# Attention probability as a difference of two exponentials, and expert routing work moved from VectorE to GpSimd, in a fused two-layer block kernel

## The reference

```python
# layer 0, attention over 7x7 windows of 8x8 tokens: every window attends to 4 windows (256 keys)
attn = einsum('bhnsd,bhnkd->bhnsk', q * scale, key_g)      # 64 queries x 256 keys, 8 heads
score, index = top_k(attn, 32)                             # the 32 best of 256 keys
out = einsum('bhnsk,bhnskd->bhnsd', softmax(score), v_sel) # + a 3x3 depthwise convolution of v
x = x + out @ out_w.T + out_b
# layer 0, experts on t = x
n = layernorm(t); probs = softmax(n @ router_w.T)
rw, re = top_k(probs, 2); rw = rw / max(rw.sum(), 1e-12)
t = t + n + sum_e combine[:, e] * (gelu(n @ w1[e] + b1[e]) @ w2[e] + b2[e])
# layer 1: 3x3 convolution of layernorm(x) with +-1 weights, then 8 experts, top 2, weights not renormalised
```

## Time and profile before

| | us |
|---|---|
| runs without profile, median of 3 | 6441.68 |
| the profiled execution's own time | 6440.11 |
| its span, first to last instruction | 6438.2 |
| VectorE busy | 5596.4 (87%) |
| TensorE matmul busy | 4737.3 (74%) |
| GpSimd busy | 4425.8 (69%) |
| ScalarE busy | 4054.4 (63%) |

### The profile page before, as it was taken

How to read it: one execution, slowest core, us unless ns; L and a number is a source line. 1 busy time by engine, 2 the same in 40 slices (tenths; PEclk the granted TensorE clock), 3 DMA queues, 4 the chain that set the end, 5 groups by cost and what they waited for, 6 DMA issues and landing times.

```text
span 6438.2 us, 135940 instructions
## 1 busy us (share of the span) xinstructions
PE 4737.3 (74%) x26938; PEld 2880.6 (45%) x26938; DVE 5596.4 (87%) x24453; ACT 4054.4 (63%) x10222; POOL 4425.8 (69%) x3986
## 2 busy tenths in 40 slices
PE   3566777777777777777777777777777777777776
PEld 1333444444444444444444444444444444444444
DVE  1999999988989998999989898989999899999941
ACT  2455666666666666666666666666666666666643
POOL 1667776767677776767677677767776777777742
PEclk9666767777777777777777777777777777777777
DMA  4111111111111111111111111111111111111100
GB/s 75 39 31 42 34 40 34 40 32 42 30 41 34 39 35 34 40 32 43 32 42 30 40 36 36 38 33 40 32 43 31 43 31 32 30 30 34 33 11 10
DMA packets 585501, 229.09 MB, mean 36 GB/s; under 512 B 481152, under 2 KB 580224, under 8 KB 584576
## 3 DMA queue, kind: packets, MB, share of 16 engines
q1 hardware_dynamic: 584576, 219.25, 15.4%
HBM read 150.14 MB, written 68.80 MB: 34 GB/s over the span
## 4 chain that ended last, share of the span: by engine, by line
PE 29%; ACT 18%; issue 16%; DVE 15%; POOL 12%; ACTq 0%; DVEq 0%; POOLq 0%; DMA 0%; SPq 0%
DVE b_v L452 7%; POOL b_r L502 5%; PE y_ps L685 4%; DVE b_r L463 4%; PE h_ps L611 4%; POOL c_h L762 4%; ACT b_x L478 3%; PE a_ps L666 3%; PE pT_ps L524 3%; PE o_ps L545 2%; ACT b_e L485 2%; ACT L737 2%; PE h_ps L666 2%; POOL b_rec L493 2%; ACT L478 2%
## 5 line engine op out<-in xcount | busy, mean ns | idle before, releaser
L463 DVE MATCH_REPLACE8 b_r<-b_v,b_r 128x256 f32<-128x256 f32 x4704 | 1879.1, 416 | 0.0
L502 POOL TENSOR_SCALAR b_r<-b_r,b_rec 128x256 f32<-128x256 f32 x1568 | 1777.1, 1147 | 119.6 <-POOL b_rec L493 119.6
L452 DVE MAX8 b_v<-b_r 128x8 f32<-128x256 f32 x4704 | 1649.2, 418 | 0.0
L524 PE MATMUL pT_ps<-k_ident,b_e 128*128 128x128 f32 x3136 | 669.9, 352 | 776.3 <-ACT b_pT L532 688.3
L493 POOL TENSOR_TENSOR b_rec<-b_den,k_mone 128x4 f32<-128x4 f32 x392 | 400.5, 1022 | 1153.5 <-ACT b_x L478 1150.2
L762 POOL TENSOR_TENSOR c_h<-c_h,c_cb 128x448 f32<-128x448 f32 x672 | 760.9, 1133 | 503.9 <-ACT c_cb L739 503.0
L524 PEld LDWEIGHTS pT_ps<-k_ident,b_e 128*128 128x128 f32 x3136 | 472.6, 180 | 1161.2 <-issue 1136.2
L510 POOL TENSOR_TENSOR b_e<-b_e,b_r 128x1024 f32<-128x1024 f32 x392 | 923.5, 2356 | 18.0 <-POOL b_r L502 14.4
L685 PE MATMUL y_ps<-k_w,c_h 128*112 128x64 f32 x5376 | 776.1, 298 | 181.1 <-POOL c_h L762 177.9
L685 PEld LDWEIGHTS y_ps<-k_w,c_h 128*112 128x112 f32 x5376 | 706.5, 210 | 404.1 <-issue 403.0
L452 DVE MAX8 b_v<-b_s 128x8 f32<-128x256 f32 x1568 | 551.1, 415 | 318.0 <-POOL b_e L510 201.2
(11 more groups left out here) (146 smaller groups left out, 7904.9 us busy)
## 6 DMA issues: line engine op xcount, KB each, us to landing
q_d<-a_qe SPq DMA_DIRECT2D x56, 448.0 KB, 4.2
b_k<-k_d SPq DMA_DIRECT2D x1568, 16.0 KB, 2.0
b_v<-v_d SPq DMA_DIRECT2D x1568, 16.0 KB, 2.0
b_q<-q_d SPq DMA_DIRECT2D x392, 64.0 KB, 2.1
c_win<-vpad_d SPq DMA_DIRECT2D x56, 145.0 KB, 2.8
c_hm<-cpad_d SPq DMA_DIRECT2D x56, 145.0 KB, 2.3
vpad_d<-a_vT SPq DMA_DIRECT2D x56, 116.0 KB, 3.7
c_win<-vpad_d SPq DMA_DIRECT2D x56, 116.0 KB, 2.7
```

The costliest lines, as they stand in the source:

```text
L452: top = dve.max(out=b_v8[p][:, t, 8 * rnd:8 * rnd + 8], in_=src[:, t, :])
L463: last = dve.match_replace(out=b_r[p][:, t, :], in_to_replace=b_v8[p][:, t, 8 * rnd:8 * rnd + 8], in_values=src[:, t, :], imm_value=GONE)
L502: last = pool.tensor_scalar(out=b_r[p][:, t, :], in0=b_r[p][:, t, :], scalar1=GONE, scalar2=b_rec[p][:, t:t + 1], op0=ALU.is_le, op1=ALU.mult)
L524: last = pe.transpose(pT_ps[:, col:col + 128], b_e[p][:, t, c * 128:(c + 1) * 128], k["ident"][:, :])
```

## The change

Five things are done.

1. In the attention, GpSimd's mask and its product go. Instead ScalarE takes the exponential also of `b_r`, in which the 32 chosen scores stand at -3e38 and so give 0 (`act_rest`, two halves of two heads), and GpSimd subtracts this from the exponential of all scores, in two halves (`pool_prob`). The division by the sum moves behind the product with v: TensorE spreads `b_rec` into 128 further columns of `o_ps`, ScalarE copies 256 columns instead of 128, and GpSimd multiplies once per strip (step NORM).
2. In the slot's order on ScalarE, `act_exp` of the next region now ends the slot, `act_turn`, `act_rest`, `act_scores`, `act_turn`, `act_sum` begin it, and the strip steps with a fraction under 0.2 stand behind these. TensorE's order follows it.
3. The sum `tok = x + pr` (step ADD) and the norm of the experts' input run on GpSimd.
4. The router on VectorE is now four MAX8 and four MATCH_REPLACE8 on 14 elements (8 logits, and 6 large fillers so that only the best two logits are replaced). GpSimd subtracts the maximum, ScalarE takes 64 exponentials a token instead of 32, and GpSimd makes the weights with ten small instructions (step 4).
5. `PLACES` moves steps accordingly.

```diff
         def dve_select(dve, tau, r):
-            dve.wait_ge(b_prob, reg + 1)
+            dve.wait_ge(b_prob, 2 * reg + 2)
+            dve.wait_ge(b_sum, reg + 1)
...
+        def act_exp(act, tau, r):
+            act.wait_ge(b_max, reg + 1)
+            act.activation(b_nm[p][:, :], b_v8[p][:, :, 0], ACT.Copy, scale=-1.0).then_inc(b_neg, 1)
+            act.wait_ge(b_neg, reg + 1)
+            for t in range(HP):
+                last = act.activation(b_e[p][:, t, :], b_s[p][:, t, :], ACT.Exp, bias=b_nm[p][:, t:t + 1])
+            last.then_inc(b_exp, 1)
+        def act_rest(act, tau, r):
+            for half in range(2):
+                act.wait_ge(b_sel, 2 * reg + half + 1)
+                for t in range(2 * half, 2 * half + 2):
+                    last = act.activation(b_r[p][:, t, :], b_r[p][:, t, :], ACT.Exp, bias=b_nm[p][:, t:t + 1])
+                last.then_inc(b_rest, 1)
...
-            for t in range(HP):
-                last = pool.tensor_scalar(out=b_r[p][:, t, :], in0=b_r[p][:, t, :], scalar1=GONE, scalar2=b_rec[p][:, t:t + 1],
-                                          op0=ALU.is_le, op1=ALU.mult)
+        def pool_prob(pool, tau, r):
+            for half in range(2):
+                pair = slice(2 * half, 2 * half + 2)
+                if half == 0:
+                    pool.wait_ge(b_exp, reg + 3)
+                pool.wait_ge(b_rest, 2 * reg + half + 1)
+                pool.tensor_tensor(out=b_e[p][:, pair, :], in0=b_e[p][:, pair, :], in1=b_r[p][:, pair, :],
+                                   op=ALU.subtract).then_inc(b_prob, 1)
...
+            for t in range(HP):
+                pe.matmul(o_ps[32 * t:32 * t + VH, 128:256], b_rec[r % 2][:, t:t + 1].broadcast_to([128, VH]), k["ident"][:, :],
+                          start=True, stop=True)
...
+            if step == NORM:
+                pool.wait_ge(b_att, NWIN * (s + 1) + 1)
+                pool.tensor_tensor(out=b_at[i][:, 0:2], in0=b_at[i][:, 0:2], in1=b_at[i][:, 2:4], op=ALU.mult).then_inc(b_nrm, 1)
+            if step == ADD:
+                pool.tensor_tensor(out=D["tok"][i][:, :, :], in0=D["x"][i][:, :, :], in1=D["pr"][:, :, :], op=ALU.add).then_inc(S["free"], 1)
...
+                for t in range(NT):
+                    ins = dve.max(out=pv[:, t, :], in_=lr[:, 0, t, :])
+                link(ins)
                 for t in range(NT):
-                    ins = dve.max_index(out=D["pi"][:, t, :], in_max=D["pv"][:, t, :], in_values=p[:, t, :])
+                    ins = dve.match_replace(out=lr[:, 1, t, :], in_to_replace=pv[:, t, :], in_values=lr[:, 0, t, :], imm_value=GONE)
+                ins.then_inc(S["top"], 1)
...
-                ("c0", 0): 78.1, ("c0", TURN): 78.5, ("c0", TURNED): 78.68, ("c0", 2): 81.66, ("c0", GATE): 82.05,
+                ("c0", 0): 78.62, ("c0", TURN): 78.7, ("c0", TURNED): 78.8, ("c0", 2): 81.66, ("c0", GATE): 82.05,
...
                     for r in range(SLOTS):
-                        if on:
-                            act_sum(act, b, r)
-                            act_exp(act, b, r)
-                        steps(act, "act", n, lo, r, fs, 0, 0.2)
                         if before:
                             act_turn(act, b, r - 1, 0)
+                        if on:
+                            act_rest(act, b, r)
                         if on and (r + 2 < SLOTS or not last):
                             act_scores(act, b, r + 2)
                         if before:
                             act_turn(act, b, r - 1, 1)
+                        if on:
+                            act_sum(act, b, r)
+                        steps(act, "act", n, lo, r, fs, 0, 0.2)
                         if before:
                             act_values(act, b, r - 1)
-                        steps(act, "act", n, lo, r, fs, 0.6, 1)
+                        steps(act, "act", n, lo, r, fs, 0.2, 1)
+                        if on and (r + 1 < SLOTS or not last):
+                            act_exp(act, b, r + 1)
```

More of the change, by code:

```diff
@@ L136, in program @@
         b_pT = [sb(f"b_pT{i}", [128, 512]) for i in range(2)]
-        b_at = [sb(f"b_at{i}", [128, 2, RH, W]) for i in range(2)]
+        b_at = [sb(f"b_at{i}", [128, 4, RH, W]) for i in range(2)]
         def buffers(n):
@@ L751, in pool_c @@
             s = tau * 2 + i
+            if step == NORM:
+                pool.wait_ge(b_att, NWIN * (s + 1) + 1)
+                pool.tensor_tensor(out=b_at[i][:, 0:2], in0=b_at[i][:, 0:2], in1=b_at[i][:, 2:4], op=ALU.mult).then_inc(b_nrm, 1)
+            if step == ADD:
+                pool.wait_ge(S["x_in"][i], LOADS[layer] * (tau + 1))
+                pool.wait_ge(S["pr"], s + 1)
+                alone(pool)
+                if layer == 1:
+                    pool.wait_ge(S["x2"], s + 1)
+                    alone(pool)
+                pool.tensor_tensor(out=D["tok"][i][:, :, :], in0=D["x"][i][:, :, :], in1=D["pr"][:, :, :], op=ALU.add).then_inc(S["free"], 1)
             if step == 1:
@@ L755, in pool_c @@
                 rstd(pool, D["mv"], D["rs"], 1e-5, S["tmp"], s, S["rstd"])
-            if step == 2 and layer == 0:
-                pool.wait_ge(S["norm"], s + 1)
-                pool.tensor_tensor(out=D["xr"][i][:, :, :], in0=D["tok"][i][:, :, :], in1=D["xn"][:, :, :], op=ALU.add).then_inc(S["res"], 1)
+                pool.wait_ge(S["rstd"], s + 1)
+                alone(pool)
+                normalise(pool, D["tok"][i], D["mv"], D["rs"], D["xn"], S["sub"], s + 1, S["norm"])
+                if layer == 0:
+                    pool.wait_ge(S["norm"], s + 1)
+                    pool.tensor_tensor(out=D["xr"][i][:, :, :], in0=D["tok"][i][:, :, :], in1=D["xn"][:, :, :], op=ALU.add).then_inc(S["res"], 1)
@@ L809, in dve_c @@
             if step == 1:
-                dve.wait_ge(S["x_in"][i], LOADS[layer] * (tau + 1))
-                dve.wait_ge(S["pr"], s + 1)
-                alone(dve)
-                if layer == 0:
-                    dve.wait_ge(S["res"], s + 1)
-                    alone(dve)
-                link(dve.tensor_tensor(out=tok[:, :, :], in0=D["x"][i][:, :, :],
-                                       in1=D["pr"][:, :, :], op=ALU.add))
-                dve.sem_inc(S["free"], 1)
+                dve.wait_ge(S["free"], s + 3)
                 mean_var(tok, mv, S["stat"])
-            if step == 2:
-                dve.wait_ge(S["rstd"], s + 1)
-                alone(dve)
-                normalise(dve, tok, mv, D["rs"], xn, S["chain"], 1, S["norm"])
             if step == 3:
@@ L826, in dve_c @@
                 alone(dve)
[L827 to L836 removed]
+                lr, pv = D["lr"], D["pv"]
@@ L1188 @@
     lay["sel_1"] = full(np.broadcast_to((expert3[:, None, None] == expert[None, :, None]), (3 * NE, NE, 128)).astype(f))
-    lay["iota"] = np.broadcast_to(expert.astype(f), (128, NE))
     lay["mhalf"] = np.full((128, NT), -0.5, f)
```

194 lines of the change are left out of this document (88 added, 106 removed).

## The result

The changed kernel takes 6919.4 us (median of 4 runs, 6918.1 to 6926.6) against 6442.3 us for the kernel before on the same chip (4 runs, 6435.7 to 6443.4): ratio 1.0745, 95% interval 1.0727 to 1.0764. It is 7.4% slower. The prediction was 6910 us.

A forecast was written before the change was run, and what follows sets the result against it. The prediction took two loops, VectorE's and ScalarE's, to bound the kernel, with ScalarE's longer after the change: 90.5 work plus 29.9 waits, 120.4 us a cycle. Phases of +397, +103 and -30 us on 6440 gave 6910; range 6400 to 7110.

The forecast's parts named there:

- What bounds the kernel: Two loops: VectorE busy 100 us a cycle, ScalarE's work and waits 105 of 110.7; the change relieves one, loads the other.
- ScalarE's work: Exponentials 11.8, four more table loads 5.1, wider `b_at` copy 0.7: 17.6 us a cycle more, 72.9 becomes 90.5.
- ScalarE's waits: Waits for TensorE, and through it GpSimd: 29.9 us a cycle after the change, where 32.4 stood.
- Slot 1: Layer 0's convolution of 8.5 us leaves 7.9 exposed on ScalarE; with the following small waits 12.8 us a cycle.
- Slot 0: `xT` waits behind the last expert's product, second matmul and transposes, 3.2; with stage a's two waits 4.5 us.
- Slot 4: Layer 1's convolution, 3.5 us, stands before the values: a 1.7 us wait, and 1.9 for `pr`, `cwT`, `xT`.
- the 2.8 twice in slots 5 and 6: The third Gelu on ScalarE waits for GpSimd's product and TensorE's second and first matmuls: 2.8 us in each slot.
- The table load's price: Each ScalarE table load costs its row, 1.283 us, without the skill's drain of about 1380 ns; four more, 5.1 a cycle.
- GpSimd at nothing: GpSimd's new small-weights chain, taken as 4.5 us, costs nothing because ScalarE's longer loop covers it.
- The phases: 276 slots at 17.2 for 15.76 us, +397; last 79 at 16.0 for 14.7, +103; first 37, -30.
- the "faster" rival: VectorE is relieved and ScalarE's waits shrink below 20 us a cycle: near 6060 or 6270 us; chance 0.15.
- What I listed to look for: ScalarE near 75% busy, VectorE idle before first maximum, some 750 loads; wrong if slot 1 or a cycle's waits under 20.

The follow-up runs named there:

- the attention half alone: Kernel before plus only the attention part, its slot order and convolution place; router, sums and norms stay on VectorE at old places: 6573.8 us, ratio 1.0224.
- the first experiment: Changed kernel with the router's exponential on ScalarE moved from between the two Gelus to behind both: 6568.6 us, ratio 1.0212.

## Why the prediction was right, step by step

- **What bounds the kernel.** Right for the changed kernel: not VectorE. It lost 1.7 us a slot (2938.43/233 = 12.6 now, 12.5 predicted) and the kernel became slower; 510 us given back to it cost 29, and between the attention half alone and the first experiment it lost 1.4 us a slot for nothing. For the kernel before, where it led at 87%, this stays argued: no run relieves VectorE there without loading GpSimd.
- **ScalarE's work.** 88.5 us a cycle for 90.5. The rest's exponentials are 394.5/33.3 = 11.8, as predicted; the loads 14.0 a cycle at 1283 ns; `b_at` 0.11 us longer for 0.1. By groups the sum rises by 17.9 us a cycle, against the 17.6 predicted; the union of all, which is the busy time, rises by only 15.6 (88.5 for 72.9). The 2 us too many are overlap at the ends of instructions, which the row of a single group doesn't show.
- **ScalarE's waits.** 31.7 us a cycle for 29.9. Slot 1: 6.58 + 0.19 + 0.73 + 0.59 + 0.69 + 0.76 + 1.91 = 11.5 for 12.8, since the convolution took 7.3 us and not 8.5. Slot 0: 3.87 + 0.21 + 2.09 = 6.2 for 4.5. `t_a` 3.4 for 2.4. Slot 4: 92/33.3 = 2.8 a cycle before `b_at`, behind layer 1's convolution, for the 1.7 foreseen. Not foreseen: 2.1 before `b_pT`, which I had as gone. Against them the Gelus wait 155.7/33.3 = 4.7, for 5.6 (the 2.8 twice in slots 5 and 6). Errors of both signs cancel, so the sum is better than its terms.
- **The table load's price.** The row, 1.28 us with nothing around it, was right for ScalarE. Removing 4 a cycle gave 6.8 us, 1.7 each: between the 1.28 of the row and the 2.66 that the Trainium skill (ScalarE: Activation LUTs, "What ACT_TABLE_LOAD costs") gives. The trace does not agree with the drain in that figure: the 466 loads have 8.2 us of idle time before them in all, and the extra stands in ScalarE's waits for TensorE.
- **The path.** The sum treats every wait on ScalarE as a fixed term. That step was too simple, though it met the number: the move that takes the wait before `yT` gives back about half of it, the rest's exponentials 40% of their length. As I read it, the sum could be right because it listed what stands in ScalarE's loop after the change, with TensorE's lateness in it. It is no price list for taking one of them out. That it came within 10 us, 0.1%, is luck in part: busy time was 2 us a cycle too high, the waits 2 too low.
- **GpSimd at nothing.** Held: it waits 1113 us for ScalarE's `b_r` in the stretch. The chain of weights takes about 4 us (4.5 predicted). The product of step NORM, 2.08 us a strip, I didn't price; it lay under the taps, and TensorE waited for it only when these went.
- **The phases.** 17.17 us a slot (17.2 predicted); 76 slots from 5400 to about 6616 us, 16.0 each (16.0 predicted); 42 in the first 539 us, 12.8 each, where the gain of half of 1.8 on 13.2 would be 12.3.
- **The range.** Its ends don't come out of its own sum: waits of 19 and 35 us a cycle give about 6360 and 7170, not 6400 and 7110. The 16 a cycle of the "faster" rival give 6290, not 6270. Nothing hangs on either.
- **What I listed to look for.** Slot 1 takes 23.4 us and the waits sum to 31.7, where under 20 would have shown me wrong; the loads are 736 for some 750. The share of ScalarE is 71%, not 75, over the run, behind TensorE and VectorE. VectorE's idle time does not stand mainly before the first maximum but before `c_st` and `c_pv`; I had not thought that its router steps would wait in order for GpSimd's sum and ScalarE's logits.

What stays open: which part of the 132 us of the attention half is the exponentials and which the new order, what layer 1's convolution costs or gives by its move alone, and whether the last wait before `b_pT` could be taken from TensorE's order. None was tried.
